# Graph attention on one core: VectorE's selection steps set apart, the sums' scan in three pieces, and another order of ScalarE's copies

## What is computed

```python
def _gatv2_layer(x, src, dst, Wl, Wr, a, b):
    xl = (x @ Wl).reshape(N, H, O)          # H = 4, O = 16
    xr = (x @ Wr).reshape(N, H, O)
    s = leaky_relu(xl[src] + xr[dst], 0.2)
    e = einsum('eho,ho->eh', s, a)
    m = segment_max(e, dst)
    ex = exp(e - m[dst])
    alpha = ex / (segment_sum(ex, dst)[dst] + 1e-16)
    return segment_sum(xl[src] * alpha[:, :, None], dst).reshape(N, H * O) + b

h = max(layernorm(x), 0)
x = x + three such layers of h (relu between them)
h = max(layernorm(x), 0)
msg = relu(h[src] + edge_attr @ W_edge.T + b_edge)     # last stage
h = h + segment_sum(msg, dst)
x = x + linear(relu(batchnorm(linear(h))))
```

## Time and profile before

| | |
|---|---|
| median of 3 runs | 7037.84 us (7034.35 to 7038.1) |
| profiled execution | 7037.6 us, span 7035.8 us |
| PE matmuls | busy 5553.2 us (79%) |
| VectorE | busy 5037.3 us (72%) |
| GpSimd | busy 4853.9 us (69%) |
| ScalarE | busy 4615.5 us (66%) |
| chain of waits that ended last | issue 34%, DVE 29%, ACT 23%, POOL 5%, PE 3% |

### The profile page before, as it was taken

How to read it: one execution, slowest core, us unless ns; L and a number is a source line. 1 busy time by engine, 2 the same in 40 slices (tenths; PEclk the granted TensorE clock), 3 DMA queues, 4 the chain that set the end, 5 groups by cost and what they waited for, 6 DMA issues and landing times.

```text
span 7035.8 us, 92697 instructions
## 1 busy us (share of the span) xinstructions
PE 5553.2 (79%) x22976; PEld 4500.0 (64%) x22976; DVE 5037.3 (72%) x7373; ACT 4615.5 (66%) x6093; POOL 4853.9 (69%) x5111
## 2 busy tenths in 40 slices
PE   0588888888838888888865888888882999999995
PEld 0466666666626777777744777777771777777773
DVE  6588888888847888888864888888885344343442
ACT  0377777777726888888853888888881555555553
POOL 2666666666667777777767777777774777777774
PEclk9988898888858999999977999999996999999996
DMA  8344445455424555555543555555552444444441
GB/s 347 108 147 147 147 147 147 147 150 150 149 78 139 155 166 155 166 155 166 156 125 94 155 166 155 165 156 165 156 164 53 136 133 136 130 133 135 130 132 45
DMA packets 419825, 1018.62 MB, mean 145 GB/s; under 512 B 162514, under 2 KB 195268, under 8 KB 415446
## 3 DMA queue, kind: packets, MB, share of 16 engines
q1 hardware_dynamic: 194242, 560.85, 23.6%
q0 software_dynamic: 164208, 181.25, 14.2%
q10 hardware_dynamic: 61348, 276.27, 9.6%
HBM read 633.43 MB, written 384.49 MB: 145 GB/s over the span
## 4 chain that ended last, share of the span: by engine, by line
issue 34%; DVE 29%; ACT 23%; POOL 5%; PE 3%; DVEq 2%; ACTq 2%; DMA 2%; SPq 0%; POOLq 0%
DVE sb_s_run L1056 11%; ACT sb_v_in L620 9%; ACT sb_turn_out L620 7%; DVE pG L1022 6%; DVE pG L1025 4%; DVE sb_wide L1009 3%; ACT sb_hot L620 3%; POOL sb_hot_f L441 3%; PE pG L529 2%; POOL marks L445 2%; ACT pB L700 2%; DVE sb_s L1221 2%; ACT sb_pick_turn L620 1%; DVE sb_XR L963 1%; DVE pG L1028 1%
## 5 line engine op out<-in xcount | busy, mean ns | idle before, releaser
L529 PE MATMUL pG<-sb_xl_parts,sb_hot 128*128 128x476 f32 x21952 | 5217.9, 397 | 1064.1 <-ACT sb_hot L620 830.3
L441 POOL DMA_INDIRECT sb_xl<-xl_table,sb_idx x4704 | 4459.3, 948 | 1751.3 <-issue 1484.5
L529 PEld LDWEIGHTS pG<-sb_xl_parts,sb_hot 128*128 128x128 f32 x21952 | 4301.6, 199 | 2020.6 <-issue 1387.3
L620 ACT ACTIVATE sb_hot<-sb_wide 128x1792 fp32r<-128x1792 bf16 x784 | 1320.0, 1697 | 583.4 <-DVE sb_wide L1009 287.4
L1022 DVE COPY_PREDICATED pG<-sb_pick_turn,pG 128x408 f32<-128x408 int32 x784 | 453.0, 578 | 1071.8 <-ACT sb_pick_turn L620 1021.8
L1056 DVE TENSOR_TENSOR_SCAN sb_s_run<-pB,sb_v_in 128x544 f32<-128x544 f32 (+1 forms) x784 | 1009.2, 1329 | 27.9 <-ACT sb_turn_out L620 22.8
L620 ACT ACTIVATE sb_turn_out<-sb_s_run 128x1088 f32<-128x1088 f32 (+1 forms) x392 | 826.7, 2109 | 8.8 <-DVE sb_s_run L1056 8.8
L620 ACT ACTIVATE sb_xl<-pG 128x136 f32<-128x136 f32 (+2 forms) x826 | 236.9, 289 | 703.5 <-DVE pG L1028 620.2
L1049 DVE TENSOR_TENSOR_SCAN pB<-sb_same_c,pB 128x1024 f32<-128x1024 f32 x294 | 674.8, 2295 | 10.1
L620 ACT ACTIVATE sb_v_in<-sb_v_g 128x1024 f32<-128x1024 f32 x291 | 600.8, 2065 | 0.0
L620 ACT ACTIVATE pB<-sb_mark 128x960 f32<-128x960 f32 x294 | 561.3, 1909 | 55.3 <-ACT sb_xr_carry L620 53.4
(11 more groups left out here) (201 smaller groups left out, 2593.3 us busy)
## 6 DMA issues: line engine op xcount, KB each, us to landing
sb_wide<-hots SPq DMA_DIRECT2D x294, 896.0 KB
state_rows<-sb_turn_out ACTq DMA_DIRECT2D x294, 576.0 KB
sb_mark<-marks SPq DMA_DIRECT2D x294, 512.0 KB, 4.3
hots<-sb_wide SPq DMA_DIRECT2D x98, 896.0 KB, 4.0
sb_xl<-xl_table,sb_idx POOLq DMA_INDIRECT x4704
marks<-sb_hot_f ACTq DMA_DIRECT2D x32, 1568.0 KB
agg_rows<-sb_turn_out ACTq DMA_DIRECT2D x98, 512.0 KB
sb_wide<-codes SPq DMA_DIRECT2D x98, 128.0 KB, 6.4
```

The costliest lines, as they stand in the source:

```text
L441: return pool.indirect_dma_start(out=dst, out_offset=None, in_=table, in_offset=bass.IndirectOffsetOnAxis(ap=index, axis=0))
L529: product = pe.matmul(pG[:, a, 0:GB * TW], hot[k][:, m, a * P:(a + 1) * P], xl_part[part][:, m * GB * TW:(m + 1) * GB * TW], start=(m == 0 ...
L620: return act.activation(out, in_, ACT.Copy)
```

## The change

On VectorE, in every attention turn but a layer's last: the three selection steps of share 0 no longer stand in a row with a wait between; `v_g` stands between the first and second, and the first column of `xr` (`begin_xr`, split off from `scan_xr`) between the second and third. The waits for masks and for TensorE's product of share 0 move ahead of `wf_arg`, that for share 1 ahead of the scan of `xr`. The sums' scan is cut into three pieces of 612, 272 and 272 elements, and the second and third step of share 1 stand between them; a layer's first turn, which has no sums, keeps the three steps in a row. The increments of `s_passed` between them are gone.

On ScalarE: masks, flags and `w_turn` stand ahead of the marks, which before came first; and at the turn's end the copy of the second share's rows stands ahead of the widening of the second half.

```diff
@@ -718,10 +718,8 @@
                 if not last:
                     act.wait_ge(s_added, turn_all + 1)
                     copy(xr_carry[:, :].unsqueeze(2), xr[:, :, G - 1:G]).then_inc(s_xr_carried, 1)
-                    act.wait_ge(s_xr_carried, l * (TURNS - 1) + turn + 1)
-                    act.sem_inc(s_passed, 1)
-                    turn_marks((use + k + 1) * 16, 1 - k)
                     turn_masks(turn + 1, 1 - k)
+                    spread_same(turn_all + 1, turn + 1)
                 else:
                     hand_out(l * TURNS + (2 * i + (k - 1)), turn - 2, k)
                     act.wait_ge(s_sums, turn_all)
@@ -733,7 +731,9 @@
                     act.wait_ge(s_v, turn_all + 1)
                     act.sem_inc(s_f, 1)
                 else:
-                    spread_same(turn_all + 1, turn + 1)
+                    act.wait_ge(s_xr_carried, l * (TURNS - 1) + turn + 1)
+                    act.sem_inc(s_passed, 1)
+                    turn_marks((use + k + 1) * 16, 1 - k)
                     rows_copied(turn_all + 2, use + k, 0, 1 - k)
                     if widened:
                         widen_turn(l, i, k, 0, fresh)
@@ -742,9 +742,9 @@
                 if not first and not second and not last:
                     hand_out(l * TURNS + (2 * i + (k - 1)), turn - 2, k)
                 if not last:
+                    rows_copied(turn_all + 2, use + k, 1, 1 - k)
                     if widened:
                         widen_turn(l, i, k, 1, fresh)
-                    rows_copied(turn_all + 2, use + k, 1, 1 - k)
 
             def attention_layer(l, fresh):
                 for g in range(GROUPS):
...
+            def select_stage(k, q, stage):
+                lo, hi = SHARES[q]
+                n = (3, 2, 1)[stage] * TW
+                at = (4, 2, 1)[stage] * TW
+                rows = pG[:, lo:hi, :]
+                return dve.copy_predicated(rows[:, :, 0:n], over(pick_turn[:, k, stage, lo:hi], n), rows[:, :, at:at + n])
...
@@ -1089,6 +1095,9 @@
                 done(dve.tensor_tensor_scan(m_run[:, k].rearrange(flat3), neg_h[:].rearrange(flat3), e_in[:, 0].rearrange(flat3),
                                             0.0, ALU.add, ALU.max)); last()
                 done(tt(e_in[:, 1, :, 1:G1], m_run[:, k, :, 0:G], neg_h[:, :, 1:G1], ALU.add)); last()
+                if not last_turn:
+                    dve.wait_ge(s_mask, turn_all + 2)
+                    dve.wait_ge(s_pg[0], turn_all + 2)
                 tt(wf_arg[:], e_in[:, :, :, 1:G1], blocks(m_run[:, k, :, 1:G1], 2), ALU.subtract).then_inc(s_args, 1)
                 xl_heads = xl[:, k, :, 0:C].rearrange("p g (h o) -> p g h o", h=H)
                 weights = over(w_turn.rearrange("p h g -> p g h"), O)
@@ -1099,16 +1108,39 @@
                     dve.wait_ge(s_used[k], use + 1)
                     attention_sums(turn_all)
                 else:
-                    select_rows(turn_all + 2, turn_all + 2, turn_all * 2 + 2, 1 - k, 0)
+                    picks = (turn_all + 1) * 4
+                    select_stage(1 - k, 0, 0).then_inc(s_pick, 1)
+                    dve.wait_ge(s_pick, picks + 1)
                     dve.wait_ge(s_w, turn_all + 1)
                     dve.wait_ge(s_v, turn_all)
                     tt(v_g[:].rearrange("p g (h o) -> p g h o", h=H), xl_heads, weights, ALU.mult).then_inc(s_used[k], 1)
+                    select_stage(1 - k, 0, 1).then_inc(s_pick, 1)
+                    dve.wait_ge(s_pick, picks + 2)
+                    begin_xr(turn_all + 1, bass.ds(turn + 1, 1), 1 - k, l * (TURNS - 1) + turn + 1)
+                    select_stage(1 - k, 0, 2).then_inc(s_sel[0], 1)
                     if build:
                         build_one_hot(i + 1, k, turn_all + 1)
-                    scan_xr(turn_all + 1, bass.ds(turn + 1, 1), 1 - k, l * (TURNS - 1) + turn + 1)
-                    select_rows(turn_all + 2, turn_all + 2, turn_all * 2 + 3, 1 - k, 1)
-                    if not first:
-                        attention_sums(before)
+                    dve.wait_ge(s_pg[1], turn_all + 2)
+                    scan_xr(turn_all + 1)
+                    select_stage(1 - k, 1, 0).then_inc(s_pick, 1)
+                    if first:
+                        dve.wait_ge(s_pick, picks + 3)
+                        dve.sem_inc(s_passed, 1)
+                        select_stage(1 - k, 1, 1).then_inc(s_pick, 1)
+                        dve.wait_ge(s_pick, picks + 4)
+                        dve.sem_inc(s_passed, 1)
+                        select_stage(1 - k, 1, 2).then_inc(s_sel[1], 1)
+                    else:
+                        third = (V - HALF * H) // 2
+                        dve.wait_ge(s_v, turn_all)
+                        dve.wait_ge(s_out, before)
+                        dve.wait_ge(s_pick, picks + 3)
+                        scan_sums(f_flat, 0, HALF * H)
+                        select_stage(1 - k, 1, 1).then_inc(s_pick, 1)
+                        dve.wait_ge(s_pick, picks + 4)
+                        scan_sums(f_flat, HALF * H, HALF * H + third)
+                        select_stage(1 - k, 1, 2).then_inc(s_sel[1], 1)
+                        scan_sums(f_flat, HALF * H + third, V).then_inc(s_sums, 1)
                 assert steps[0] == K_TURN, steps[0]
 
             def attention_layer(l, build):
```

More of the change, by code:

```diff
@@ L1018, in select_rows @@
                 dve.sem_inc(s_passed, 1)
-                lo, hi = SHARES[q]
-                mask = [pick_turn[:, k, stage, lo:hi] for stage in range(3)]
-                rows = pG[:, lo:hi, :]
-                dve.copy_predicated(rows[:, :, 0:3 * TW], over(mask[0], 3 * TW), rows[:, :, 4 * TW:7 * TW]).then_inc(s_pick, 1)
+                select_stage(k, q, 0).then_inc(s_pick, 1)
                 dve.wait_ge(s_pick, selects * 2 + 1)
                 dve.sem_inc(s_passed, 1)
-                dve.copy_predicated(rows[:, :, 0:2 * TW], over(mask[1], 2 * TW), rows[:, :, 2 * TW:4 * TW]).then_inc(s_pick, 1)
+                select_stage(k, q, 1).then_inc(s_pick, 1)
                 dve.wait_ge(s_pick, selects * 2 + 2)
                 dve.sem_inc(s_passed, 1)
-                dve.copy_predicated(rows[:, :, 0:TW], over(mask[2], TW), rows[:, :, TW:2 * TW]).then_inc(s_sel[q], 1)
+                select_stage(k, q, 2).then_inc(s_sel[q], 1)
             def cut_parts(g, base):
@@ L1037, in cut_parts, with begin_xr @@
                 cp(xl_part[1][:, sl], left).then_inc(s_parts, 1)
-            def scan_xr(turn_all, turn, k, carried):
+            def begin_xr(turn_all, turn, k, carried):
                 dve.wait_ge(s_xrin, turn_all + 1)
@@ L1045, in scan_xr @@
                                          op0=ALU.mult, op1=ALU.add).then_inc(s_xr_begun, 1)
+            def scan_xr(turn_all):
                 dve.wait_ge(s_xr_begun, turn_all + 1)
@@ L1049, in scan_xr, with scan_sums @@
                 dve.tensor_tensor_scan(xr_flat, same_c[:].rearrange(flat3), xr_flat, 0.0, ALU.mult, ALU.add).then_inc(s_xr, 1)
-            def scan_sums(turn_all, factors, halves):
-                dve.wait_ge(s_out, turn_all)
-                for lo, hi in halves:
-                    n = (hi - lo) * G1
-                    ins = dve.tensor_tensor_scan(s_run[:, lo:hi, :].rearrange(flat3), factors[:, 0:n],
-                                                 v_in[:, lo:hi, :].rearrange(flat3), 0.0, ALU.mult, ALU.add)
-                ins.then_inc(s_sums, 1)
+            def scan_sums(factors, lo, hi):
+                return dve.tensor_tensor_scan(s_run[:, lo:hi, :].rearrange(flat3), factors[:, 0:(hi - lo) * G1],
+                                              v_in[:, lo:hi, :].rearrange(flat3), 0.0, ALU.mult, ALU.add)
             def attention_sums(turn_all):
                 dve.wait_ge(s_v, turn_all + 1)
-                scan_sums(turn_all, f_flat, ((0, HALF * H), (HALF * H, V)))
+                dve.wait_ge(s_out, turn_all)
+                scan_sums(f_flat, 0, HALF * H)
+                scan_sums(f_flat, HALF * H, V).then_inc(s_sums, 1)
             def linear_sums(turn_all):
-                scan_sums(turn_all, same_half, ((0, C // 2), (C // 2, C)))
+                dve.wait_ge(s_out, turn_all)
+                scan_sums(same_half, 0, C // 2)
+                scan_sums(same_half, C // 2, C).then_inc(s_sums, 1)
             def attention_turn(l, i, k, first=False, last_turn=False, build=False):
@@ L1125, in attention_layer @@
                 dve.sem_inc(s_passed, 1)
-                scan_xr(l * TURNS, slice(0, 1), 0, None)
+                begin_xr(l * TURNS, slice(0, 1), 0, None)
+                scan_xr(l * TURNS)
                 for q in range(len(SHARES)):
```

## The result

The changed kernel takes 7544.74 us (median of 4 runs, 7541.36 to 7547.18) against 7037.47: 7.2% slower, ratio 1.0721 with a 95% interval of 1.0703 to 1.074. The loss is 507 us where 382 were predicted, a time of 7420; the measured time is inside the range of 7310 to 7550, 5 us from its upper end. The profiled execution has a span of 7539.5 us, 503.7 more than before.

What follows compares the result with a forecast made beforehand. It saw GpSimd nearly full (1470 of 1481 us, second layer) and expected the ring to set the changed turns. 95 turns x 1.40 x 2 layers plus 95 x 1.22 gave +382 us, so 7420; range 7310 to 7550.

Steps and rivals of the forecast that it cites:

- the ring: Attention turn: closed loop of VectorE and ScalarE steps, max copy to max copy, 16.69 us against 15.29; 88 in 100.
- turns of 16.7 and 18.6 us: Expected turn lengths: 16.69 us in the second and third layer, 18.65 us in the first.
- `lr` to the end of the arguments: VectorE, early in the turn: from `lr` to the end of the softmax arguments, 3.70 us.
- `w` to the marks: ScalarE's middle: gap between `w` and the marks, taken as 0.15 us, between 0.10 and 0.40.
- end of the marks to the first row of `xr`: ScalarE to VectorE, before share 0's third step: handover of 0.13 us.
- from row copy to widening: ScalarE: the widening follows 0.18 us after the row copy.
- the high bounds: Upper limits, 0.25 us at `w`, 0.25 at the marks, up to 0.4 in joints: +0.45 a turn, 7550 us.
- The tail of pieces: VectorE's turn end: two sums pieces and share 1's steps 2 and 3, 2.66 us plus 0.10 for joints.
- The savings beside the ring: VectorE: mask wait 0.74 us and four selection gaps of 0.15, 1.3 us a turn, kept from the end by the hand-out.
- The slow second block of TensorE: Rival: second matmul block slowed by the clock to 9.1 us, sums 2.3 us late, 7860 us; 4 in 100.
- The faster: Rival: VectorE's waits simply go, second and third layer stop at GpSimd's limit, 6890 us; 5 in 100.
- the unchanged case: Rival: savings and the longer turn loop cancel, 7030 to 7050 us; 3 in 100.

Runs made afterwards that it cites:

- b_middle_3: Kernel before with only ScalarE's middle in the new order (masks, flags, w, marks), whole gather, chip without stall: 6917.78 us, ratio 0.9826.
- half of the gather: Both kernels and two variants, 14 matmuls per share instead of 28: before 6988.47, changed 7478.82, changed with old ScalarE tail 7185.74, before with new middle 6894.44 us.
- b_middle: Kernel before with only ScalarE's middle in the new order, on a chip where TensorE stalls: 9424.97 us, ratio 0.9999.
- a_sums_back: Changed kernel with VectorE's share 1 selection in a row again before the sums' scan, on a stalling chip: 9237.55 us, ratio 0.9804 to the kernel before.
- a_middle_back: Changed kernel with ScalarE's middle in its old order (marks, masks, w, flags), on a stalling chip: 9302.2 us, ratio 0.9869 to the kernel before.

## Why the prediction was right, point by point

- **The mechanism.** The signs of the ring that it named are there: the second widening starts 0.22 us after the third step of share 1 (2649.53 to 2649.75) and overlaps the `s` add at 2650.07; the factor wait is 129.4 us in 96 turns over the whole layer (130 or more were said); the sums' first piece waits 1.6 us in 94 of the 95 turns that have a hand-out; the mask wait is gone; GpSimd waits for `v_g`. Only the turns of 16.7 and 18.6 us that it named came out longer.
- **The size was too small.** +382 was predicted, +507 came: turns of 17.14 us in the second layer ((1660.1 - 14.6) / 96) instead of 16.69, and 18.94 instead of 18.65 in the first. The longer turns make some 113 us of the 125 missing; most of the rest is a layer's first turn, which the sum left as it was and which takes 14.6 us instead of 12.5 in the second and third layer, and one turn a layer that the sum did not count. The terms of the sum that were mis-sized, from the turn above: `lr` to the end of the arguments 3.86 us, not 3.70, as `wf_arg`, which now has three waits, starts 0.19 us after the step ahead of it, where the gap was 0.03 (2501.96 to 2501.99 before); `w` to the marks 0.25 (0.33 in the turn before), not 0.15; end of the marks to the first row of `xr` 0.34, not 0.13; from row copy to widening 0.26 (0.18 in the turn before), not 0.18. That is 0.55 us together; a few hundredths less elsewhere make it the 0.51 by which this turn of 17.20 us is longer than the sum. The hand-out 2.13 and its handover 0.12 were right. In the first layer the same gaps were smaller: 0.17 from `w` to the marks (1004.09 to 1004.26) and 0.21 from their end to the first row of `xr` (1006.19 to 1006.40). That the result is still inside the range, by 5 us, is in part luck: the high bounds lay at `w`, at the marks and in the joints, and for the gap ahead of the first row of `xr` and for `wf_arg` there was none.
- **The tail of pieces** was right in sum: first piece to the end of the third step 2.72 us (2646.81 to 2649.53) against 2.76 with the allowance. But a piece of 272 elements takes 0.72 us, not 0.60; against it the 0.10 allowed for the joints was not needed, and the two steps took 0.42 and 0.28 instead of 0.45 and 0.30.
- **The savings beside the ring.** The prediction had the masks' 0.74 us hidden by the ring; b_middle_3 shows that this edit without the others is worth 122 us. Its estimate for such a gain (at most 11 us in the second and in the third layer, up to GpSimd's limit) was too low: 30.1 us in the third. The 0.32 us of issue in front of a gather, which it took as fixed, fell to 0.30 (238.6 / 783).
- **The rivals.** The slow second block of TensorE did not come. Kernel after, second layer, timeline of PE:

```profile
2627.43 7.85 PE L529 MATMUL pG<-sb_xl_parts,sb_hot 128*128 128x476 f32 x28 [2.91 <-ACT sb_hot L620]
...
2635.43 6.30 PE L529 MATMUL pG<-sb_xl_parts,sb_hot 128*128 128x476 f32 x28
```

The first block of a turn, after 2.91 us of idle, ran at a granted 0.78, between the levels of 1.2 and 2.4 GHz; the second followed at once and ran at 1.00, the upper level, in 6.30 us. The scan of `xr` waits for a block in 16 turns, 8.5 us in all. The kernel before had such slow blocks in its second layer too (7.70 us at 2491.68, after 2.77 us idle), beside the fast one of the earlier trace rows. The prediction set the 1.0 us gap against the Trainium skill, "TensorE: Matmul & The Clock Gate", section "HAM oscillation — how this bites in real kernels"; that section speaks of long gaps alone, so the gap doesn't contradict it. The faster and the unchanged case are excluded.
- **Which part of the change costs what** is settled with half of the gather: VectorE's new order 291 us, the swapped tail 293, the new middle order a gain of 94, together the 490. The ring with the swapped tail in it and the wait for the hand-out are both in the prediction; that VectorE's part costs about as much as the tail, through two steps inside the scan, is not split out there. How VectorE's 291 us divide between the two shares was not run where TensorE doesn't stall; that `v_g` and the first row of `xr`, which now stand ahead of the third step of share 0, make it 0.86 us later is read from the order.

By the first part of what the Trainium skill says in "VectorE: DVE Perf Modes", section "The DRAIN you can't avoid", the joints without a wait would have overlapped nothing. In the turn above, piece 1 ends at 2648.24 and step 2, which waits for nothing, starts at 2648.16: the 0.08 us of overlap is there, and of the section's two parts this kernel shows the second, that an operation which isn't held starts earlier.

## What to carry to other kernels

Filling short gaps of the busiest engine puts its last step later, and whatever another engine has queued behind that step goes late with it; ask for each moved step who copies its result and what stands behind that copy. Here gaps of 0.15 us were filled, and a 1.70 us widening that had been free came to stand behind the last step. And a step that is moved from ahead of a wait to behind it is no longer hidden: two steps moved behind the wait for the hand-out made the scan 0.74 us longer and brought it no earlier. Of a change in several parts, time the parts alone: one of these is worth 1.7% without the others.

## What the runs showed of the hardware

On two of the chips TensorE stood still once in nearly every turn of the layers (96 times in the 97 turns of b_middle's second layer), for some 6 us each time and longer in the last stage, without waiting for another engine of the core. b_middle there, last stage, timeline of all engines:

```profile
8018.05 0.71 SPq L354 DMA_DIRECT2D sb_wide<-hots  x1
...
8020.35 0.20 ACT L620 ACTIVATE sb_pick_turn<-sb_pick 128x12 int32 x1
...
8027.07 0.94 POOL L441 DMA_INDIRECT sb_xl<-xl_table,sb_idx  x1 [0.30 <-issue]
8032.28 1.69 PEld L529 LDWEIGHTS pG<-sb_xl_parts,sb_hot 128*128 128x128 f32 x5 [15.71 <-issue]
8032.31 0.59 DVE L1022 COPY_PREDICATED pG<-sb_pick_turn,pG 128x408 f32<-128x408 int32 x1 [19.84 <-remote]
8032.31 1.92 PE L529 MATMUL pG<-sb_xl_parts,sb_hot 128*128 128x476 f32 x4 [15.34 <-remote]
```

ScalarE has been done since 8020.55, GpSimd since 8028.01, the block of share 0 since 8016.97; then, after 15.34 us, TensorE's next block and the selection step that waits for the last one start together. Up to 250 us into the program, before the loops, the engines' busy times are the same as on the other chips. By the program, the one semaphore that both of the instructions starting at 8032.31 wait for is the one that share 0's product raises when it is done (`pe_gathered0`), and the trace's record of it has it raised at 8032.18. So TensorE waits for the completion of its own block, whose end in the timeline is worked out by the profile, not recorded. In the kernel before, on a chip that doesn't stall, that record comes 0.01 us after the block's end (2482.49 and 2482.50). Why it comes so late here stays open. Open too is why the variants of the changed kernel were 1.3 to 2.4% faster than the kernel before there. In the second layer the stall is 5.7 and 5.9 us a turn in the two runs with the tail undone and 5.9 in a_sums_back, against 6.6 and 6.5 in the two runs of the kernel before with the new middle; in a_middle_back it is 6.5 as well, but TensorE is busy for less there, 1354 us in the layer against 1392 in b_middle. What sets either isn't known. A verdict of such a chip does not carry over: there the three variants of the changed kernel that ran win, and where TensorE doesn't stall the changed kernel loses 7% and its variant with the middle undone 9%.
